# Residual graph network: gathered tiles' halves on GpSimd and a ring for XW, and a beginning with x in two transfers, norms by logarithm and exponential, and the path chosen while x arrives

## The reference, cut to what matters

```python
# layer 0
norms = jnp.maximum(jnp.linalg.norm(x, axis=-1), COS_EPS)
sim = x @ x.T / (norms[:, None] * norms[None, :])
attn = softmax(beta * sim * adj, axis=1)
out0 = adj_norm @ x - x + sigmoid(alpha) * (attn @ x - x)
x = layernorm(x + out0)
# layer 1
XW = x @ W;  s_col = XW @ a[0, :f];  s_row = XW @ a[0, f:]
den = exp(leaky_relu(s_row[:, None] + s_col[None, :], 0.01))
num = adj @ den
att = where(num != 0, den / num, 0)
x = layernorm(x + adj @ (att @ XW))
```

## Time and profile before

| | |
|---|---|
| median of 3 runs | 685.43 us (684.15 to 686.16) |
| the profiled execution | 685.51 us, its span 683.7 us |
| PE busy | 575.0 us (84%) |
| DVE busy | 549.3 us (80%) |
| POOL busy | 428.3 us (63%) |
| ACT busy | 351.4 us (51%) |

### The profile page before, as it was taken

One profiled execution on the slowest core, in us unless ns is written; L12 is line 12 of the kernel. 1 busy time (PEld: TensorE's weight loads), 2 busy tenths in 40 slices (PEclk: granted clock), 3 DMA queues, 4 the chain that ended last, 5 costly groups with the idle time before them and its releaser, 6 DMA issues.

```text
span 683.7 us, 11037 instructions
## 1 busy us (share of the span) xinstructions
PE 575.0 (84%) x4123; PEld 356.0 (52%) x4123; DVE 549.3 (80%) x1000; ACT 351.4 (51%) x556; POOL 428.3 (63%) x448
## 2 busy tenths in 40 slices
PE   0389999999998879999529987889989988848993
PEld 0245545555452868888518643334444443427883
DVE  1669999999997763678796877899998999985442
ACT  2335444444443513679977137777867877711000
POOL 5849999999999033455305176775777676003663
PEclk9999999999999589999757999999999999997998
DMA  9999890000000000000000031333333332000110
GB/s 146 104 108 108 143 376 3 1 0 1 1 1 3 4 0 16 25 16 18 16 1 24 18 113 46 93 89 86 90 90 90 86 82 81 1 5 9 32 29 16
DMA packets 17793, 37.17 MB, mean 54 GB/s; under 512 B 2570, under 2 KB 8222, under 8 KB 17726
## 3 DMA queue, kind: packets, MB, share of 16 engines
q0 software_dynamic: 7392, 24.32, 19.8%
q1 hardware_dynamic: 10334, 11.98, 5.4%
HBM read 48.72 MB, written 10.45 MB: 87 GB/s over the span
## 4 chain that ended last, share of the span: by engine, by line
PE 41%; POOL 22%; DVE 21%; ACT 8%; issue 5%; DMA 1%; DVEq 0%; POOLq 0%; ACTq 0%; SPq 0%
POOL R L403 21%; PE PSALL L1706 8%; PE PSALL L1604 7%; PE PSALL L1419 6%; DVE ring L1233 4%; PE PSALL L1665 4%; PE PSALL L1533 3%; ACT AW L590 3%; DVE ring L1226 3%; PE PSALL L1345 2%; PE PSALL L1612 2%; ACT R L687 2%; DVE FR L1233 2%; PE PSALL L1478 1%; PE PSALL L1442 1%
## 5 line engine op out<-in xcount | busy, mean ns | idle before, releaser
L403 POOL TENSOR_TENSOR R<-R,ring 128x452 f32<-128x452 f32 (+1 forms) x126 | 170.3, 1388 | 2.4 <-ACT ring L531 2.4
L531 ACT ACTIVATE ring<-ring,sm 128x452 f32<-128x452 f32 (+1 forms) x132 | 84.8, 667 | 102.9 <-DVE ring L836 102.7
L841 DVE TENSOR_TENSOR R<-ring 128x452 bf16<-128x452 f32 (+1 forms) x88 | 106.1, 1206 | 0.0
L1345 PE MATMUL PSALL<-XN 128*128 128x452 f16 (+2 forms) x396 | 99.2, 362 | 4.2 <-issue 4.2
L461 POOL DMA_INDIRECT AW<-ATd,FR x44 | 63.8, 1451 | 61.3 <-PE PSALL L1612 36.2
L1604 PE MATMUL PSALL<-AW,R 128*128 128x452 fp8e4 (+1 forms) x348 | 77.6, 354 | 24.9 <-DVE R L1165 18.6
L836 DVE TENSOR_TENSOR ring<-PSALL,AT 128x452 f32<-128x452 f32 (+1 forms) x132 | 78.6, 616 | 4.7 <-PE PSALL L1345 4.3
L1665 PE MATMUL PSALL<-ring,X 128*128 128x452 bf16 (+1 forms) x300 | 67.8, 360 | 0.9 <-DVE ring L1233 0.9
L1345 PEld LDWEIGHTS PSALL<-XN 128*128 128x128 f16 (+1 forms) x396 | 37.6, 98 | 56.7 <-issue 25.1
L1604 PEld LDWEIGHTS PSALL<-AW,R 128*128 128x128 bf16 x348 | 31.9, 97 | 64.6 <-DVE R L1165 26.8
L1233 DVE TENSOR_TENSOR ring<-ring 128x904 bf16<-128x904 f32 (+1 forms) x50 | 62.5, 1250 | 0.0
(11 more groups left out here) (252 smaller groups left out, 1083.5 us busy)
## 6 DMA issues: line engine op xcount, KB each, us to landing
AT<-in_adjT POOLq DMA_DIRECT2D x22, 338.5 KB, 26.4
ATd<-AT SPq DMA_DIRECT2D x2, 3723.5 KB, 16.8
XWd<-ring SPq DMA_DIRECT2D x11, 128.0 KB, 1.8
out<-ring SPq DMA_DIRECT2D x21, 64.0 KB, 1.5
AW<-ATd,FR POOLq DMA_INDIRECT x44, 4.3
X<-XWd,idx POOLq DMA_INDIRECT x22, 3.1
Wt<-in_W SPq DMA_DIRECT2D x1, 64.0 KB, 11.2
X<-in_x SPq DMA_DIRECT2D x1, 0.5 KB, 8.0
```

The costliest lines, as they stand in the source:

```text
L403: i = G.tensor_tensor(ES_, ES_, z, ALU.add)
L531: S.activation(z, z, ACT.Exp, scale=bcol[0:rows, :]).then_inc(s_exp, 1)
L841: V.tensor_tensor(Fl[q % 6][0:rows, 0:w], ring[0:rows, q % 6, 0:w], upper(q, rows, w), ALU.subtract).then_inc(s_low, 1)
L1345: m = TE.matmul(PSALL[0:rows, b, 0:w], lh[:, jt * P:jt * P + rows], rh[:, c0:c0 + w], start=(k == 0), stop=(k == 2))
```

## The change

**Beginning.** Beta and alpha are now fetched first, and x comes in two transfers of 11 tiles. Squares and sums are made in four parts (`QT`). The norm's reciprocal is made by ACT's logarithm and exponential with one correction on DVE (four small instructions); the power on POOL is gone, and POOL instead waits for x before its 18 transfers of `AT`. The flag is made between the sums and the correction. ACT scales the rows of groups 1 and 4 (four instructions each); the transposes use four banks; the chain of the scale is spread between the groups. The logits wait only for the groups that they read. Of `xl`, POOL makes the first four tiles before the attention and the other 18 inside it, behind the sixth copy (`low_rest`).

**Loop.** POOL makes the lower halves of the gathered tiles (`halves`), and DVE only the table's (`sums_half`). Scores, exponentials and halves of the second gathered tile are made only where `kind` is 1, so that DVE, ACT and POOL each read `win` and branch once a tile. The split of XW takes two instructions instead of three and writes a ring of four places (`XW2`), so that it waits for PE's product of the tile four before. On POOL a tile's order is now: rows, halves, XW, split.

```diff
-            q(X3, x.rearrange("(t p) d -> p t d", p=P)).then_inc(s_x, 16)
+            q(braw, beta.broadcast_to([P, 1])).then_inc(s_beta, 16)
+            q(araw, alpha.broadcast_to([P, 1])).then_inc(s_beta, 16)
+            for h in range(2):
+                q(X3[:, h * 11:(h + 1) * 11, :],
+                  x[h * 11 * P:(h + 1) * 11 * P, :].rearrange("(t p) d -> p t d", p=P)).then_inc(s_x[h], 16)
...
-            gp.wait_ge(s_sq, 2)
-            G.tensor_tensor(nrm, sq, half.broadcast_to([P, T]), ALU.pow).then_inc(s_norm, 1)
+            for h in range(2):
+                gp.wait_ge(s_x[h], 16)
             for t in range(4, T):
                 load_AT(t)
             gp.wait_ge(s_xh, 1)
-            G.tensor_tensor(xl[:, 4:T, :], X3[:, 4:T, :], xh[:, 4:T, :], ALU.subtract).then_inc(s_xlrest, 1)
+            G.tensor_tensor(xl[:, 0:4, :], X3[:, 0:4, :], xh[:, 0:4, :], ALU.subtract).then_inc(s_xlfirst, 1)
+
+            def low_rest():
+
+                G.tensor_tensor(xl[:, 4:T, :], X3[:, 4:T, :], xh[:, 4:T, :], ALU.subtract).then_inc(s_xlrest, 1)
...
+                    if (jt, c) == (0, NC - 1):
+                        low_rest()
...
             def split_xw(t):
-                gp.wait_ge(s_ohl[0], T)
-                gp.wait_ge(s_perm[0], 1)
                 gp.wait_ge(s_AT[t], 32)
-                if t:
-                    gp.wait_ge(s_xws, 3 * t)
-                G.tensor_copy(iota[:, :], XWs[:, t, :]).then_inc(s_xws, 1)
-                gp.wait_ge(s_xws, 3 * t + 1)
-                G.tensor_tensor(XWh[:, t, :, 0], XWs[:, t, :], iota[:, :], ALU.subtract).then_inc(s_xws, 1)
-                gp.wait_ge(s_xws, 3 * t + 2)
-                G.tensor_copy(XWh[:, t, :, 1], iota[:, :]).then_inc(s_xws, 1)
+                if t >= 4:
+                    gp.wait_ge(s_y, 3 * (t - 3))
+                G.tensor_copy(XW2[:, t % 4, 1, :], XWs[:, t, :]).then_inc(s_xws, 1)
+                gp.wait_ge(s_xws, 2 * t + 1)
+                G.tensor_tensor(XW2[:, t % 4, 0, :], XWs[:, t, :], XW2[:, t % 4, 1, :], ALU.subtract).then_inc(s_xws, 1)
...
-            for jt in range(2, T):
-                if jt + 4 < T:
-                    fetch_xw(jt + 4)
-                split_xw(jt)
+            def halves(jt):
+
+                s = T + jt % 2 * DS
+                kind = eng.value_load(win[0:1, jt:jt + 1], min_val=0, max_val=2)
+                gp.wait_ge(s_dene, jt + 1)
+                met = gp.covered()
+                with eng.If(kind == 1):
+                    G.tensor_tensor(den_h[:, s + 1:s + DS, :, 0], den_w[:, s + 1:s + DS, :], den_h[:, s + 1:s + DS, :, 1],
+                                    ALU.subtract).then_inc(s_denb, 1)
+                gp.only(met)
+                with eng.Else():
+                    G.tensor_tensor(den_h[:, s + 1, :, 0], den_w[:, s + 1, :], den_h[:, s + 1, :, 1], ALU.subtract).then_inc(s_denb, 1)
+            def layer1(general):
+
+                for jt in range(2, T):
+                    fetch_rows(jt)
+                    if not general:
+                        halves(jt - 1)
+                    if jt + 4 < T:
+                        fetch_xw(jt + 4)
+                    split_xw(jt)
+                if not general:
+                    halves(T - 1)
...
-            av.wait_ge(s_x, 16)
-            for t0, nt in ((0, 11), (11, 11)):
-                S.activation(xx[:, t0:t0 + nt, :], X3[:, t0:t0 + nt, :], ACT.Square).then_inc(s_square, 1)
-            for g, (t0, nb) in enumerate(GRP):
+            av.wait_ge(s_beta, 32)
+            S.activation(eal, araw, ACT.Exp, scale=-1.0).then_inc(s_ealpha, 1)
+            for h, (t0, nt) in enumerate(QT):
+                av.wait_ge(s_x[h // 2], 16)
+                S.activation(xx[:, t0:t0 + nt, :], X3[:, t0:t0 + nt, :], ACT.Square).then_inc(s_early, 1)
+            av.wait_ge(s_sq, 5)
+            S.activation(deg, sq, ACT.Ln).then_inc(s_norm, 1)
+            av.wait_ge(s_norm, 1)
+            S.activation(rn, deg, ACT.Exp, scale=-0.5).then_inc(s_norm, 1)
+
+            def normal_rows(g):
+
+                t0, nb = GRP[g]
+                av.wait_ge(s_sq, 6)
+                for t in range(t0, t0 + nb):
+                    i = S.activation(AO3[:, t, :], X3[:, t, :], ACT.Copy, scale=rn[:, t:t + 1])
+                i.then_inc(s_early, 1)
+
+            def rows_high(g):
+
+                t0, nb = GRP[g]
                 av.wait_ge(s_xnT, g + 1)
-                S.activation(xnh[:, t0 * P:(t0 + nb) * P], PSALL[:, g % 2, 0:nb * P], ACT.Copy).then_inc(s_xnh, 1)
+                S.activation(xnh[:, t0 * P:(t0 + nb) * P], PSALL[:, g % 4, 0:nb * P], ACT.Copy).then_inc(s_xnh, 1)
+
+            normal_rows(1)
+            rows_high(0)
+            normal_rows(4)
+            for g in range(1, 6):
+                rows_high(g)
             S.activation(xh, X3, ACT.Copy).then_inc(s_xh, 1)
-            av.wait_ge(s_w, W_IN)
-            S.activation(eal, araw, ACT.Exp, scale=-1.0).then_inc(s_ealpha, 1)
...
+                kind = eng.value_load(win[0:1, jt:jt + 1], min_val=0, max_val=2)
                 av.wait_ge(s_denz, 3 * (jt + 1))
                 s = T + jt % 2 * DS
-                S.activation(den_w[:, s:s + DS, :], den_w[:, s:s + DS, :], ACT.Exp).then_inc(s_dene, 1)
+                met = av.covered()
+                with eng.If(kind == 1):
+                    S.activation(den_w[:, s + 2, :], den_w[:, s + 2, :], ACT.Exp)
+                av.only(met)
+                S.activation(den_w[:, s:s + 2, :], den_w[:, s:s + 2, :], ACT.Exp).then_inc(s_dene, 1)
...
+            dv.wait_ge(s_sq, 4)
+            V.tensor_scalar(sq, sq, COS_EPS * COS_EPS, None, ALU.max).then_inc(s_sq, 1)
+            dv.wait_ge(s_beta, 32)
+            V.tensor_scalar(bcol, braw, 1.0 / (XS * XS), None, ALU.mult).then_inc(s_bcol, 1)
+            V.tensor_copy(flag[:, :], beta2).then_inc(s_flag, 1)
+            dv.wait_ge(s_norm, 2)
+            k = own.step(V.tensor_tensor(dis, rn, rn, ALU.mult))
...
+            V.scalar_tensor_tensor(rn, dis, XS, rn, ALU.mult, ALU.mult).then_inc(s_sq, 1)
+            dv.wait_ge(s_sq, 6)
...
+            normal_rows(0)
+            k = own.step(V.scalar_tensor_tensor(nrm, sq, 1.0 / (XS * XS), rn, ALU.mult, ALU.mult))
+            normal_rows(2)
+            dv.wait_ge(s_dve, k)
             V.tensor_reduce(pm, nrm, AX.X, ALU.max).then_inc(s_pm, 1)
-            scale_of(0, (PSALL[0:1, 5, 0:P], PSALL[:, 5, 0:1]), XS, up_x, down_x)
+            rows_low(0)
+            normal_rows(3)
+            dv.wait_ge(s_scale, 1)
+            k = own.step(V.tensor_reduce(top, PSALL[0:1, 5, 0:P], AX.X, ALU.max))
+            rows_low(1)
+            dv.wait_ge(s_dve, k)
+            V.tensor_scalar(top, top, 1e-30, None, ALU.max).then_inc(s_top, 1)
+            normal_rows(5)
+            rows_low(2)
+            rows_low(3)
+            dv.wait_ge(s_scale, 2)
+            k = own.step(V.tensor_scalar(down_x, PSALL[:, 5, 0:1], XS * 2.0 ** -14, None, ALU.mult))
+            rows_low(4)
+            dv.wait_ge(s_dve, k)
+            V.reciprocal(up_x, down_x).then_inc(s_up, 1)
+            rows_low(5)
             dv.wait_ge(s_ealpha, 1)
             k = own.step(V.tensor_scalar(eal, eal, 1.0, None, ALU.add))
...
+            sig_ok = own.step(V.reciprocal(sig, eal))
+            dv.wait_ge(s_dve, sig_ok)
+            dv.wait_ge(s_iota, 2)
...
+            def small_scores(jt, usual):
                 dv.wait_ge(s_pick, 2 if jt < FIRST else 4)
+                if usual:
+                    kinds[jt] = eng.value_load(win[0:1, jt:jt + 1], min_val=0, max_val=2)
+                    met = dv.covered()
+                    with eng.If(kinds[jt] == 1):
+                        score(jt, 1)
+                    dv.only(met)
+                    score(jt, 0).then_inc(s_denz, 2)
+                else:
+                    for q in range(WN):
+                        score(jt, q).then_inc(s_denz, 1)
                 V.tensor_scalar(den_w[:, s, :], cb3[:, jt, :], e_bias[:, jt:jt + 1], e_cap, ALU.add, ALU.min).then_inc(s_denz, 1)
-                for q in range(WN):
-                    V.tensor_scalar(den_w[:, s + 1 + q, :], cb3[:, jt, :], Rw[:, q, jt:jt + 1], r01w[:, q, jt:jt + 1],
-                                    ALU.add, ALU.max).then_inc(s_denz, 1)
...
+                sums_half(jt)
+
+            def sums_half(jt):
+
+                s = T + jt % 2 * DS
+                dv.wait_ge(s_dene, jt + 1)
                 V.tensor_tensor(den_h[LOROWS:P, s, :, 1], den_w[LOROWS:P, s, :], den_h[LOROWS:P, s, :, 1],
                                 ALU.subtract).then_inc(s_denb, 1)
...
                             if cp == 0:
-                                small_scores(jt + 1)
+                                small_scores(jt + 1, True)
                             if cp == 1:
-                                small_halves(jt + 1)
+                                sums_half(jt + 1)
...
+            turn(0)
+            turn(1)
+            pe.wait_ge(s_pm, 1)
```

(64 more changed lines are left out.)

78 lines of the change are left out of this document (37 added, 41 removed).

## The result

| | before | after |
|---|---|---|
| median (16 runs each, same chip) | 686.49 us | 679.68 us |
| lowest to highest | 683.36 to 688.29 | 677.87 to 683.09 |
| ratio, 95% interval | | 0.991, 0.989 to 0.993 |

The change makes the kernel 6.2 to 6.8 us faster, where 15.5 were forecast. The sign and the loop's mechanism were right; the time lies 0.7 us above the range. The loop gained what was forecast and a little more. The beginning, from which 8.5 us should have come, costs some 2.5, because the second half of x lands at 23.4 us and not at 9.9.

The account below looks back on a forecast made before the run. POOL's additions were taken to bound the attention, DVE the loop's kind 0 tiles and PE its kind 1 tiles. From 685.5 us, 8.5 for the beginning and 7.0 for the loop were taken off: 670.0 us, range 662 to 679.

Parts of the forecast that it names:

- What bounds the kernel: POOL's additions set the attention's pace; in the loop DVE bounds kind 0 tiles (8.39 of 8.46 us), PE kind 1.
- The step that failed: Beginning, norms: x's second half lands at 9.9 us, from 8.87 + 0.94 and a little for four `AT` transfers.
- The bad end of 11: Beginning: the latest landing allowed for x's second half, 11 us, part of the 6 us bound on the beginning's gain.
- Or the halves of x arrive together, at 11: 671.1: Beginning: both halves of x land at 11 us, total 671.1 us, counted within the forecast; no chance of its own.
- The rest of the beginning: Rows start at 14.0, POOL's first copy at 26.0, additions at 37.3 us; whole beginning gains 8.5 us, 6 to 11.
- DVE blocked: Attention: during `low_rest` (5.04 us) DVE's two-input SBUF instruction may stand still, exponentials then missing for about 1.3 us.
- the 6 us end: Beginning: lower bound of its gain, 6 us, with x at 11, DVE fully blocked for 5 us and two units lost.
- Loop, DVE and POOL: Loop: DVE's kind 0 tile falls from 8.46 to 7.7 us; 0.5 gained at each of 14 waits, 7 us.
- POOL's delay: Loop: POOL's tile of 8.4 us exceeds DVE's 7.7, so POOL is late by some tenths in kind 0 runs.
- The 7.05 for PE's own work: Loop, kind 0 tile: PE's own work is 8.46 less at most 1.43 of waiting, 7.05 us, so DVE sets the pace.
- rival 1: Loop: POOL becomes the bound, 8.4 against 7.7 us; the loop gains about 2.5 us, total 674.5; chance 0.20.
- Rivals 2 and 3: Loop, DVE's load and branch: not hidden, 677.0, chance 0.12; or branches cost more than a load, 695.6, chance 0.07.

Follow-up runs that it names:

- adj_behind_x: The changed kernel, but POOL waits for both halves of x before issuing its first four `AT` transfers; 668.06 us, ratio 0.973 to before.
- loop_only: The kernel before with the loop's part of the change alone; 677.31 us, ratio 0.987 to before.
- before_small_two: The kernel before with x in two transfers and beta and alpha ahead of x in SP's queue; 700.24 us, ratio 1.020 to before.
- loop_both_scores: loop_only with both scores made in every tile on DVE, without the load of `kind` and branch there; 680.09 us, ratio 0.991 to before.

## Why the prediction was wrong, step by step

**What bounds the kernel** was read rightly. What moved at the attention's end came back in the time: POOL's memset behind it is 10.2 us earlier than before in adj_behind_x, which is 9.2 us faster than loop_only (same loop, old beginning), and 14.8 later in before_small_two, which is 14.3 slower than before.

**The step that failed** is "the second, which I put at 9.9 (8.87 + 0.94 and a little for the four `AT` transfers that it meets; 11 is the bad end)". It was 23.4. I had taken the landing of the earlier trace rows and shifted it by the issue times, as if the transfer kept its speed. The same row held for one transfer with large packets, and neither the packets' size nor the order of SP's and POOL's queues was priced. The bad end of 11 was a guess with no row behind it; 11.37 is what it is with one transfer. That one step made 13.5 us at x's landing, and the first copy came 13.1 later than forecast (39.09 against 26.0). In the time the beginning is 11.0 us short of its forecast (2.5 lost, 8.5 forecast), and the loop's 1.9 above its own hid a part of that. "Or the halves of x arrive together, at 11: 671.1" named the right place as a rival, with a price twelve us too small.

**The rest of the beginning** held, measured from there. From the second half to the first scaled rows 4.2 us (23.42 to 27.60) against 4.1 forecast; from the rows to DVE's first product 10.1 against 10.4, and to POOL's first copy 11.5 against 12.0. `low_rest` took 4.55 against 5.04. From first copy to first addition 9.7 against 11.3, where the earlier trace rows had 7.46. The attention with `low_rest` in it is 188.4 - 184.6 = 3.8 us longer, forecast 13.5 - 8.5 = 5.0. With x at 10.46 the beginning gives 677.31 - 668.06 = 9.2 us; forecast 8.5.

**DVE blocked.** Of the two ends I had named, the rule of the Trainium skill's "SBUF — State Buffer" (who interferes with whom) gives the one that happened: DVE's L930, two SBUF inputs, 0.62 us just before, took 4.77 and ended just behind POOL's 4.55; PE stood 2.96 for it. It cost less than the 6 us end said: the attention grew by 3.8, which is less than `low_rest` itself, so idle time behind it was made up.

**Loop, DVE and POOL**: forecast 7.0, measured 8.7 in the trace and 8.9 in loop_only. The edits on DVE were sized a little too large (0.8 a tile, measured 0.26 + 0.43), POOL's delay much too large (0.3 a wait, measured nearly none). POOL's tile was put at 8.4 us with its gaps; it is 6.8 busy, and in 7.9 us from one half to the next (541.05 to 548.95) it still waits 0.42 for ACT, so it needs some 7.5. The 7.05 for PE's own work should have been 8.46 - 1.43 = 7.03, which changes nothing. Groups of POOL in the loop of after, 410 to 590 us, beside the earlier trace rows:

```profile
L505 POOL TENSOR_TENSOR R<-R 128x128 bf16<-128x128 f32 x15 | 20.3, 1351 | 31.5 <-ACT R L740 31.5
L463 POOL DMA_INDIRECT X<-XWd,idx x16 | 15.5, 967 | 2.4
L481 POOL CAST XW<-X 128x128 bf16<-128x128 f32 x20 | 9.1, 457 | 0.0
```

POOL waits for ACT 31.5 us in 15 tiles and is not late: rival 1 is refuted. It is close, though. In the tile at 541 us

```profile
540.37 0.41 ACT L740 ACTIVATE R<-R 128x256 f32<-128x256 f32 x1
...
541.05 1.51 POOL L505 TENSOR_TENSOR R<-R 128x128 bf16<-128x128 f32 x1 [0.37 <-ACT R L740]
...
542.36 0.35 DVE L1275 TENSOR_TENSOR R<-R 32x128 bf16<-32x128 f32 x1
...
542.77 0.94 PE L1729 MATMUL PSALL<-AW,R 128*128 128x452 fp8e4 x4 [0.71 <-DVE R L1275]
```

POOL's half ends at 542.56, DVE's at 542.71: the half on DVE is the later one by 0.15.

**Rivals 2 and 3** (load and branch on DVE): refuted by loop_both_scores: with the load and the branch taken away and the score back the kernel is 2.8 us slower, not faster. **The range** reached to 679 because rival 1 gave 674.5 and rival 2 677; the case that happened, a good loop and no beginning, was not among the cases at all, though a loss of the whole beginning with an average loop makes 678.5.

What stays open: why the clock falls ahead of the loop in most profiles and not in all; what makes x's packets small; and how much of x may be left at POOL's first data before its landing jumps. Only issues at 0.80 and 1.73 were measured, with 0.08 and 0.28 MB left.

## What to carry to other kernels

A transfer's landing time read from a trace belongs to its issue time, its packets' size and whatever shares the DMA engines with it; whoever splits it or puts something ahead of it may keep none of the three. To foresee it, ask how much of it is left when the other queue's data begin to move. Where small packets meet another queue with large ones, put the small ones first or hold the large ones back: here moving four transfers behind x, or two tiny ones, was worth some 11 us, more than one and a half times the whole change. And test the two parts of a change alone: the loop's 9 us hid that the beginning had become slower.

## What the runs showed of the hardware that I had not expected

Two queues took turns packet by packet, whatever the packets' size (254 of 0.4 KB to 253 of 2.4 KB in 6 us). The small packets' transfer then landed only when the other queue had run dry (23.4 to 23.7 us in four kernels, POOL's data ending by 23). Two transfers of 704 KB made packets of 0.5 KB, one of 1408 KB packets of 2 KB, from the same rows in DRAM. A transfer of 0.5 KB issued at 4.57 us landed at 15.6 in that company, and at 5.6 ahead of it. POOL's first `AT` data moved at 8.5 us in after and at 7.0 in small_behind_x, though the four transfers were issued from 3.54 on: what has moved by then decides.
